# The sources that are compared lie in one run of 384 elements instead of three runs of 128

## What is computed

```python
def reference(x, src, dst, etypes, weight):       # x [3125, 64], weight [16, 64, 64]
    h = x[src]                                    # [103125, 64]
    m = zeros(103125, 64)
    for r in range(16):
        m += where(etypes == r, 1.0, 0.0)[:, None] * (h @ weight[r])
    y = x + segment_sum(m, dst, 3125)
    return (y - mean(y)) / sqrt(var(y) + 1e-5)    # over the 64 features
```

## Time and profile before

| | |
|---|---|
| median of 3 runs | 871.02 us (870.95 to 871.26) |
| span of the profiled execution | 870.6 us |
| PE busy | 684.9 us, 79% |
| VectorE busy | 598.9 us, 69% |
| ACT busy | 585.6 us, 67% |
| POOL busy | 591.7 us, 68% |
| gathers (line 286) | 620, 945 ns each |
| picks on VectorE (line 464) | 1240, 402 ns each |

### The profile page before, as it was taken

The page is one execution under the profiler, slowest core; times in us unless marked ns, Lnnn a source line. Parts: engine busy times, 40 slices in busy tenths (PEclk is TensorE's granted clock), DMA queues, the critical chain, the costliest instruction groups (busy, mean ns, idle before and its releaser), DMA issues.

```text
span 870.6 us, 24502 instructions
## 1 busy us (share of the span) xinstructions
PE 684.9 (79%) x8136; PEld 643.7 (74%) x8137; DVE 598.9 (69%) x2220; ACT 585.6 (67%) x1326; POOL 591.7 (68%) x634
## 2 busy tenths in 40 slices
PE   0004998888889888888898888889888888898894
PEld 0004888787878877887887788779877887798784
DVE  0146886767677776777678668766876687678754
ACT  1307777776777677677777777677777677777732
POOL 2005777777777777777777777777777777777760
PEclk9999899999999999999999999999999999999996
DMA  1022222222222222222222222222222222222211
GB/s 63 38 88 64 71 74 69 69 63 72 69 66 66 69 72 63 69 69 71 64 66 72 69 63 69 71 70 61 71 69 72 60 72 69 71 61 69 54 46 39
DMA packets 30272, 57.46 MB, mean 66 GB/s; under 512 B 11402, under 2 KB 19402, under 8 KB 30258
## 3 DMA queue, kind: packets, MB, share of 16 engines
q0 software_dynamic: 19840, 40.67, 19.6%
q1 hardware_dynamic: 9102, 15.55, 5.0%
q10 hardware_dynamic: 1316, 1.06, 0.4%
HBM read 54.84 MB, written 2.40 MB: 66 GB/s over the span
## 4 chain that ended last, share of the span: by engine, by line
POOL 61%; issue 25%; SPq 5%; DMA 4%; PE 2%; ACT 1%; DVE 1%; POOLq 0%; DVEq 0%; ACTq 0%
POOL rows L286 61%; DMA src_b<-in_src 4%; SPq L218 2%; SPq L217 2%; PE own L686 1%; ACT away L374 1%; DVE outT L571 1%; PE own L825 0%; PE rel L736 0%; PE agg L724 0%; POOLq L194 0%; DMA rows<-x_parts,gidx 0%; ACT pick L380 0%; DVE x_sb L600 0%; ACT krel L404 0%
## 5 line engine op out<-in xcount | busy, mean ns | idle before, releaser
L286 POOL DMA_INDIRECT rows<-x_parts,gidx x620 | 586.0, 945 | 244.0 <-issue 188.0
L686 PE MATMUL own<-xp,pick 125*128 125x192 bf16 x4650 | 412.8, 253 | 82.5 <-issue 74.6
L686 PEld LDWEIGHTS own<-xp,pick 125*128 125x128 bf16 x4650 | 397.2, 101 | 93.9 <-issue 83.9
L464 DVE TENSOR_SCALAR pick<-src_h,node 125x384 bf16<-125x384 f16 x1240 | 401.9, 402 | 8.4 <-ACT src_h L342 8.4
L528 DVE TENSOR_SCALAR onehot<-ramp,krel 128x112 bf16<-128x112 bf16 x806 | 149.4, 262 | 49.6 <-issue 49.6
L374 ACT ACTIVATE away<-src_h,node_neg 125x384 bf16<-125x384 f16 x310 | 169.6, 613 | 0.1
L380 ACT ACTIVATE pick<-away,one 125x384 bf16<-125x384 bf16 x310 | 163.0, 610 | 0.0
L724 PE MATMUL agg<-onehot,rows 128*128 128x112 bf16 x2418 | 139.8, 215 | 29.1 <-DMA rows<-x_parts,gidx 23.8
L724 PEld LDWEIGHTS agg<-onehot,rows 128*128 128x128 bf16 x2418 | 122.4, 99 | 48.2 <-issue 48.1
L388 ACT ACTIVATE rows<-own 128x192 bf16<-128x192 f32 x186 | 61.4, 330 | 138.9 <-PE own L686 131.7
L736 PE MATMUL rel<-aggT,w_pair 128*64 128x64 f32 x992 | 128.7, 298 | 0.0
(11 more groups left out here) (62 smaller groups left out, 72.6 us busy)
## 6 DMA issues: line engine op xcount, KB each, us to landing
src_b<-in_src SPq DMA_DIRECT2D x62, 187.5 KB
rows<-x_parts,gidx POOLq DMA_INDIRECT x620
x_parts<-xp SPq DMA_DIRECT2D x1, 812.5 KB
x_parts<-xp SPq DMA_DIRECT2D x1, 750.0 KB
out<-x_sb SPq DMA_DIRECT2D x2, 250.0 KB
x_sb<-in_x ACTq DMA_DIRECT2D x1, 406.2 KB
src_i<-in_src SPq DMA_DIRECT2D x1, 396.5 KB
dst_i<-in_dst SPq DMA_DIRECT2D x1, 396.5 KB
```

Of the source, the lines that this page charges most:

```text
L286: pool.indirect_dma_start(rows[:, u, j, :], None, x_parts, bass.IndirectOffsetOnAxis(ap=gidx[:, u, j:j + 1], axis=0)).then_inc(rows_in[u] ...
L464: v.tensor_scalar(pick[u][:, b, :], src_h[u][:, :, 0:CUTW[u]], node[:, b:b + 1], None, ALU.is_equal).then_inc(pick_ready[u], 1)
L686: return nc.tensor.matmul(own[h][:, 0:SPLIT * D], pick[u][:, b, h * P:(h + 1) * P], xp[:, b, 0:SPLIT, :].rearrange("p s d -> p (s d)"), st ...
```

## The change

CUT becomes 1. CUTW becomes 384 and OWNW stays 384. `src_h` is now one piece of 384 elements with a GAP of 2 behind it, where it was three pieces of 128 with a GAP of 2 behind each. The same values are computed by the same number of instructions; `ramp` and its gaps stay.

```diff
-    CUT = 3
+    CUT = 1
     CUTW = [-(-n * P // (2 * CUT)) * 2 for n in OWN]
     OWNW = [CUT * w for w in CUTW]
     GAP = 2
```

## The result

The changed kernel takes 1091.39 us (median of 5 runs, 1084.6 to 1102.31) against 870.95 us before (870.18 to 871.26). The ratio is 1.250, with a 95% interval of 1.245 to 1.255; it leaves out the longest run of the change, a slow one. The forecast was 936 us. The time lies in its range of 885 to 1150 us, but the loss is 220 us where I had put 65.

The account below looks back on a forecast made before the run. POOL's unresting gathers were taken to bound the kernel. The span of 870.6 us, plus 65 us of gathers delayed by faster picks, plus 0.4 us from span to median, gave 936 us, range 885 to 1150 us.

Parts of the forecast that it names:

- What bounds the kernel: POOL's gathers of line 286 never rest: 945 ns plus a 0.30 us gap each, 12.45 us for a stage's ten.
- The pace of a pick: On VectorE, picks start every 0.23 instead of 0.324 us; twenty take 4.5 us, 124 us less busy time, worth nothing.
- ACT: Abs of line 374 gains at most 3 ns each, 1 us in all, off the chain; conversions of line 342 nothing.
- That faster picks hit the gathers: On POOL, gathers beside a burst of faster picks wait for a way into SBUF that VectorE holds; 23 to 105 us.
- The remainder of 0.82 us: Two slowed gathers of the earlier trace ended 0.81 and 0.83 us after a two-input VectorE instruction (line 556) ended.
- My upper bound: While picks and gathers alternate, a gather costs 0.74 us more, 2.3 per burst: 1.7 us a stage, 105 us, giving 976.
- the first point: A gather's first access to something VectorE held, some 0.12 us after its start, where it waits until VectorE lets go.
- The price: What faster picks cost POOL's gathers: the middle between the bounds, 1.05 us a stage, 62 x 1.05 = 65 us.
- the alternating picture: Gathers and picks take turns within a burst, costing 0.36 to 1.7 us a stage: 894 to 976 us; chance 0.46.
- shut out altogether: Rival: overlapping picks block POOL until the twentieth ends, 3.9 to 4.5 us a stage, 1111 to 1150 us; chance 0.26.
- PE's clock: Rival: longer waits for gathers halve PE's clock for some 6 us each stage, PE sets pace: 1000 to 1060 us; chance 0.09.
- VectorE held: Rival: a running gather holds the way, picks pass only in 0.30 us gaps; over 1050 us, mostly above 1150; chance 0.04.

Follow-up runs that it names:

- h3_wait_each: The changed kernel (CUT = 1) with VectorE waiting for the end of each pick before starting the next; 876.9 us where before took 872.6.

## Why the prediction was right or wrong

**What bounds the kernel: right.** The gap before a gather stayed 0.30 us, POOL waited for "issue" 613 times of 620, and the time in gathers accounts for the whole difference (224.3 of 223.1 us of span).

**The pace of a pick: right.** Forecast were a distance of 0.23 us, a duration near 300 ns and a burst of 4.5 us. Measured were 4.67 / 20 = 0.233 us, 313 ns and 4.67 us. VectorE's busy time fell from 598.9 to 488.3 us, 111 us where 124 were forecast, and bought nothing, as said: even with half the gathers gone, the faster picks gained nothing (797.9 against 791.1 us).

**ACT: right.** The Abs still takes 613 ns, the conversion 513 against 512 ns.

**That faster picks hit the gathers: right, in place and direction.** The remainder of 0.82 us after VectorE's last held instruction, read from the two gathers of the earlier trace rows, returned in the long gathers. What I had not seen is the second point, 0.13 us before a gather's end. My upper bound let all of the 0.82 us behind the first point be held up; between the two points the trace shows a gather going on beside a burst.

**The price: wrong, and this is the step that failed.** The term was 1.05 us a stage, the middle between the ends of one picture, in which picks and gathers alternate (the middle of 0.36 and 1.7 is 1.03, 1 us less in the sum). Measured were 224.3 / 62 = 3.6 us. The picture was wrong, not its middle: even its upper end, 1.7 us, is under half of what came. In most bursts the gather waited not for the next pick's end but for the twentieth's. The timeline of the changed kernel shows this, and two runs show that it takes the unbroken row: with an onehot between the picks the loss is 19.5 us, with a pause it is 4.4. That the time fell between 885 and 1150 us is no merit of the alternating picture, which ended at 976.

**The rival "shut out altogether", with 0.26, is what happened in 54 of 62 bursts**, at 1091 us where it gave 1111 to 1150. It stands 20 us under that rival's range because eight bursts are shared, where the gathers lose 0.1 to 1 us each, and because in some others a gather passed before the next was shut out. Where a gather is shut out for the whole burst, it loses 5.1 - 0.94 = 4.2 of the 4.67 us, between the 3.9 and 4.5 of the working. A hint lay in the earlier trace rows: picks of 402 ns start every 324 ns, so there is never a moment without one. I named it and gave it too little weight against "one instruction is not twenty". It was no more than a hint: rows of shorter picks overlap as well and are shared. No row of before could show where the limit in length lies.

The Trainium skill (SBUF — State Buffer, section "Who interferes with whom") has VectorE's two-port instruction hold the shared pair for its whole length and the other side blocked. For a single pick the trace of h3_wait_each agrees: the gather of 439.39 us waited for the pick's end and ended 0.81 us after it. For rows the runs show both outcomes: rows of 192 to 352 elements mostly let a gather through with 0.04 to 0.2 us of delay, rows of 384 and 768 mostly let none through.

**PE's clock: right that it would not decide.** The granted clock averaged 0.85 and the products of line 686 took 9.28 us in the stage at 508 us, where the earlier trace rows has 6.36, but POOL waited for PE 1.5 us in all.

**VectorE held: not as the cause.** That rival gave over 1050 us, so the time alone would fit it. The picks do not: the twenty of a burst took 4.67 us, as forecast for picks that nobody holds, with a mean of 313 ns. Held picks do exist, but they are few: in the changed kernel 28 of 1240 picks took 340 to 545 ns, 19 of them in the eight shared bursts, which took 4.66 to 4.96 us. In h3_wait_each 360 picks took over 450 ns. The undisturbed 1.82 us of line 556, on which I had ruled it out, does not speak for picks.

## What to carry to other kernels

A faster form of a VectorE instruction is no gain in itself: ask which engine it can stop, and whether that engine has any idle time. If GpSimd issues gathers without rest beside long unbroken rows of such instructions, either keep the slow form or put something between them; one other instruction or a wait for the last one took most of the loss away here, and so did instructions of 352 elements or fewer. And when a row shows that something waits for the end of an instruction, look whether the instructions of the row that you price overlap, and treat "until the last of them" as a case of its own. Where the loss is a matter of which engine comes first, look also at the moment at which the row begins.

## What the runs showed of the hardware that I had not expected

- The loss does not grow evenly with the length of an instruction. Unbroken rows of 192, 320 and 352 elements cost 19.1, 26.8 and 20.8 us over the whole kernel (one run each), rows of 384 cost 220.4, and half as many instructions of 768 cost 160.8.
- The same burst in the same execution can go either way: 54 of the 62 bursts hold a gather of over 2 us (41 gathers took 5.0 to 5.5 us), and eight let gathers pass at 1.04 to 1.9 us. All six that began 0.57 to 0.73 us after the start of a gather are among the eight.
- The holding goes both ways: a gather waits for a pick's end, and a pick that meets the end of a gather took 0.51 instead of 0.32 us.
- A source of two pieces with a gap (CUT = 2) is in the fast form as one piece is; three pieces with a gap are not.
- The same kernel before took 871 to 873 us in four of the six sets and 1367 and 1391 us in two, whose traces show PE stopping between matmuls. A set of each kind ran on chip 0, so that the chip decides is not shown. In the two sets kernels with the fast pick and shut-out gathers were 3.4 to 3.8% quicker than their control. A verdict on a change to POOL's work holds for the condition in which it was measured only.
